# Two attention layers on one core: the layer norms' inverse root as one power on GpSimd

## What is computed

```python
def _ln(x, g, b):
    m = jnp.mean(x, axis=-1, keepdims=True)
    v = jnp.var(x, axis=-1, keepdims=True)
    return (x - m) * jax.lax.rsqrt(v + EPS) * g + b      # EPS = 1e-05

x = _attn(_ln(x, g1, b1), _ln(x, g1, b1), Wq1, Wk1, Wv1, Wo1, bo1) + x
x = _attn(_ln(x, g2, b2), context, Wq2, Wk2, Wv2, Wo2, bo2) + x
x = _geglu_ff(_ln(x, g3, b3), Wp, bp, Wf, bf) + x
```

## Time and profile before

| | |
|---|---|
| median of 3 runs | 3316.51 us (3315.87 to 3318.76) |
| the profiled execution | 3324.0 us, span of its instructions 3322.2 us |
| PE busy | 3117.0 us (94% of the span) |
| DVE busy | 2268.7 us (68%) |
| ACT busy | 1806.2 us (54%) |
| POOL busy | 1168.2 us (35%) |
| mean granted TensorE clock | 0.961 |

### The profile page before, as it was taken

The page is one execution under the profiler, slowest core; times in us unless marked ns, Lnnn a source line. Parts: engine busy times, 40 slices in busy tenths (PEclk is TensorE's granted clock), DMA queues, the critical chain, the costliest instruction groups (busy, mean ns, idle before and its releaser), DMA issues. The chain is left out here.

```text
span 3322.2 us, 48072 instructions
## 1 busy us (share of the span) xinstructions
PE 3117.0 (94%) x16972; PEld 1824.9 (55%) x16972; DVE 2268.7 (68%) x4098; ACT 1806.2 (54%) x3369; POOL 1168.2 (35%) x621
## 2 busy tenths in 40 slices
PE   7989997999989999999999999699888799999989
PEld 5744445788635555555555488543667444444357
DVE  5557873444567777777777465599664799999844
ACT  4445553444434444444444444378655288888864
POOL 2047771000058777877787701012210000000000
PEclk9989998999989999999999999899998699999999
DMA  6989968999976676667666522434726623333140
GB/s 235 346 221 243 244 188 290 361 354 347 294 176 141 149 161 158 148 148 161 158 148 147 195 80 109 165 104 130 261 97 214 208 74 108 92 105 95 58 149 26
DMA packets 367127, 588.79 MB, mean 177 GB/s; under 512 B 47152, under 2 KB 197216, under 8 KB 365736
## 3 DMA queue, kind: packets, MB, share of 16 engines
q1 hardware_dynamic: 361844, 582.43, 59.1%
q10 hardware_dynamic: 5044, 3.29, 0.4%
HBM read 344.19 MB, written 241.29 MB: 176 GB/s over the span
## 5 line engine op out<-in xcount | busy, mean ns | idle before, releaser
L2501 ACT ACTIVATE a_prob<-a_ring 128x512 f32<-128x512 f32 (+1 forms) x1088 | 551.2, 616 | 383.9 <-PE a_ring L2418 371.0
L2266 DVE TENSOR_REDUCE a_blk_max<-a_ring 128x1 f32<-128x402 f32 x992 | 502.1, 569 | 268.8 <-PE a_ring L2257 267.9
L1966 ACT ACTIVATE a_prob<-a_ring 128x512 f32<-128x512 f32 (+1 forms) x1088 | 582.3, 605 | 135.3 <-PE a_ring L1888 130.0
L2365 POOL TENSOR_TENSOR a_prob_sum<-a_prob,a_prob_sum 128x1024 f32<-128x1024 f32 x256 | 604.1, 2399 | 0.0
L2011 DVE TENSOR_REDUCE a_blk_max<-a_ring 128x1 f32<-128x402 f32 x1024 | 506.7, 567 | 33.4 <-PE a_ring L1875 26.6
L2434 PE MATMUL a_pv<-a_prob,a_v 128*64 128x512 f32 (+1 forms) x2176 | 508.6, 606 | 0.0
L2417 PE MATMUL a_ring<-a_q_stack,a_k_stack 128*128 128x512 f32 (+1 forms) x1088 | 454.2, 417 | 18.1 <-issue 12.1
L2418 PE MATMUL a_ring<-a_q_second,a_k_second 65*128 65x512 f32 (+1 forms) x1088 | 435.8, 401 | 0.0
L2365 POOL TENSOR_TENSOR a_prob_sum<-a_prob 128x1024 f32<-128x1024 f32 x128 | 302.7, 2375 | 310.7 <-DVE a_chunk_sum L2558 199.8
L1906 PE MATMUL a_pv<-a_prob,a_v 128*32 128x256 f32 (+2 forms) x4096 | 340.7, 406 | 13.7 <-ACT a_prob L1966 7.8
L1875 PE MATMUL a_ring<-a_k_stack,a_q_stack 63*128 63x402 f32 (+1 forms) x1280 | 281.8, 423 | 37.2 <-DMA a_q_stack<-q_lo_self 17.1
(11 more groups left out here) (278 smaller groups left out, 4875.0 us busy)
## 6 DMA issues: line engine op xcount, KB each, us to landing
a_k_stack<-k_hi_cross SPq DMA_DIRECT2D x96, 400.5 KB, 4.6
a_v<-v_cross SPq DMA_DIRECT2D x48, 768.0 KB
a_k_stack<-k_lo_cross SPq DMA_DIRECT2D x80, 400.5 KB, 5.9
a_k_second<-k_hi_cross SPq DMA_DIRECT2D x32, 801.0 KB, 12.4
v_cross<-p_v_sb SPq DMA_DIRECT2D x48, 512.0 KB
k_hi_cross<-p_split_hi SPq DMA_DIRECT2D x120, 200.0 KB, 3.5
k_lo_cross<-p_split_lo SPq DMA_DIRECT2D x120, 200.0 KB, 4.8
a_q_stack<-q_hi_self SPq DMA_DIRECT2D x64, 256.0 KB, 4.4
```

What stands on the lines that cost most here:

```text
L1966: nc.scalar.activation(prob[0:keys, tau % RC, m, :], ring[0:keys, score_place(e) % BANKS, :], ACT.Exp, scale=a.scale).then_inc(exp_done, 1)
L2266: return nc.vector.reduce_max(dst, bank[:, 0:a.blk], AX.X)
L2365: nc.gpsimd.tensor_tensor(prob_sum[:, h], prob_of(i * NCP + cp, h), other, ALU.add)\
L2501: nc.scalar.activation(prob_of(w, h)[0:keys, ch % 2, :], ring[0:keys, score_bank(e), :], ACT.Exp, scale=a.scale).then_inc(exp_done, 1)
```

## The change

VectorE's reciprocals and ScalarE's square roots are left out of every normalisation. VectorE still adds EPS; GpSimd then waits for that and raises each half of `var` to the power -0.5, with the exponent read from a column of constants, and VectorE's scaling waits for GpSimd's power under the same semaphore (`rooted`) as before. In p0 `fill_constants` now follows the powers of batch 1, where it followed the row sums; in p2 `pad_values` follows the powers of the first normalisation. The exponent column is set in the setup.

```diff
-        self.den_pick = self.sbuf("den_pick", [P, 4], F32)
+        constants = self.sbuf("constants", [P, 5], F32)
+        self.den_pick, self.neg_half = constants[:, :4], constants[:, 4:5]
...
             nc.gpsimd.memset(pr.mean_ones[:], 1.0 / DIM)
+            nc.gpsimd.memset(pr.neg_half, -0.5)
...
                         nc.gpsimd.tensor_tensor(var[:, half], sq[:, 0, half], sq[:, 1, half], ALU.add).then_inc(row_sums, 1)
+                elif kind == "scale":
+                    pool.wait_ge(d_read, d_no["var", m, b] + 1)
+                    for half in HALVES:
+                        nc.gpsimd.tensor_tensor(var[:, half], var[:, half], pr.neg_half.to_broadcast([P, NQ // 2]), ALU.pow)\
+                            .then_inc(rooted, 1)
                     if fill and b == 1:
                         fill_constants()
-            pool.wait_ge(row_sums, 4 * B)
+            pool.wait_ge(rooted, 2 * B)
...
-                elif kind == "scale":
-                    for n, half in enumerate(HALVES):
-                        act.wait_ge(inverted, 2 * b + n + 1)
-                        nc.scalar.activation(var[:, half], var[:, half], ACT.Sqrt).then_inc(rooted, 1)
...
                     nc.vector.tensor_scalar(var[:], d_bank(step), EPS, None, ALU.add).then_inc(d_read, 1)
-                    dve.wait_ge(d_read, d_no[step] + 1)
-                    for half in HALVES:
-                        nc.vector.reciprocal(var[:, half], var[:, half]).then_inc(inverted, 1)
```

```diff
-                elif geglu and kind == "scale" and ln_no[m, b] == 0:
-                    pad_values()
+                elif kind == "scale":
...
+                    if geglu and ln_no[m, b] == 0:
+                        pad_values()
```

More of the change, by code:

```diff
@@ L204, in _ @@
             nc.gpsimd.memset(pr.mean_ones[:], 1.0 / DIM)
+            nc.gpsimd.memset(pr.neg_half, -0.5)
             nc.gpsimd.memset(pr.ident[:], 0.0).then_inc(const_step, 1)
-            nc.gpsimd.memset(pr.den_pick[:], 0.0).then_inc(const_step, 1)
+            nc.gpsimd.memset(pr.den_pick, 0.0).then_inc(const_step, 1)
             pool.wait_ge(const_step, 2)
@@ L209, in _ @@
                                     base=0, pattern=[[-1, P]], channel_multiplier=1).then_inc(const_step, 1)
-            nc.gpsimd.affine_select(out=pr.den_pick[:], in_=pr.den_pick[:], compare_op=ALU.not_equal, fill=1.0,
+            nc.gpsimd.affine_select(out=pr.den_pick, in_=pr.den_pick, compare_op=ALU.not_equal, fill=1.0,
                                     base=-16, pattern=[[-32, 4]], channel_multiplier=1).then_inc(const_step, 1)
@@ L288, in wide_projection @@
     HALVES = [slice(0, NQ // 2), slice(NQ // 2, NQ)]
-    centred, squared, inverted = sem("centred"), sem("squared"), sem("inverted")
+    centred, squared = sem("centred"), sem("squared")
     rooted, scaled = sem("rooted"), sem("scaled")
@@ L984, in feed_phase @@
     x_summed, centred = sem("x_summed"), sem("centred")
-    squared, inverted, rooted, scaled = sem("squared"), sem("inverted"), sem("rooted"), sem("scaled")
+    squared, rooted, scaled = sem("squared"), sem("rooted"), sem("scaled")
     z_hi_done, z_done = sem("z_hi_done"), sem("z_done")
@@ L1480, in _ @@
                         nc.scalar.activation(sq[:, :, half], xc[:, :, half], ACT.Square).then_inc(squared, 1)
[L1481 to L1484, removed]
                 elif kind == "shift":
```

## The result

The changed kernel takes 5372.75 us (median of 4 runs, 5367.96 to 5378.07) against 3317.64 us for the kernel before beside it: a ratio of 1.6175 (95% interval 1.6151 to 1.62). The forecast was 3306.5 us, and its range ended at 3385. The profiled execution has a span of 5367.0 us; the one of before had 3322.2.

What follows compares the result with a forecast made beforehand. TensorE, busy for most of the span, was taken as the bound. Gains of 8.1 us and 5.1 of clock, less 3.5 lost on chains, were rounded to 10: from 3316.5 to 3306.5 us, range 3288 to 3385.

Steps and rivals of the forecast that it cites:

- the price t: Time of one GpSimd power on a 128x256 half, taken as 2.1 us, between 0.74 and 6.1.
- rival 1: The power is long, t about 6: 74 us above the forecast, 3380; slower by over 0.2% had 0.34 in all.
- the formula: In each normalisation's chain, z_lo ends D + 2t + 0.1 + 3.5 us behind the sum with epsilon.
- the v copy: p3 at 2371: a table load and two roots leave from ahead of it, gain 2.0 us, plus 3.4 of clock.
- the mean behind p_x: p3 at 2472: VectorE's residual p_x stands behind the scaling and TensorE waits for its mean; loss 1.1 us.
- the gate: p3 at 2524: a Sqrt load, two roots and a Gelu load leave from ahead of it, gain 2.4 us.
- the second place of 1.1: p3, some 50 us before the place at 2472: the same loss of 1.1 us once more, without slack for TensorE.
- rival 3: The power is as quick as an add, t = 0.74: 25 us gained, 3291.5 us; chance 0.14.
- The loads: p2 to p4: some 35 of ScalarE's table loads for Sqrt and Gelu go, 45 us, mostly hidden behind TensorE.
- The moved fill: p0 at 41.6: the two Wv remainders meet an idle GpSimd, gain 2.6 us, plus 1.7 of clock.
- The port: VectorE instructions with two SBUF operands wait until GpSimd's present instruction ends, so scaling starts at 2t; otherwise 0.83 us less.
- D: VectorE's two-operand instructions between sum and scaling: about 1.1 us for one weight's remainder or two u remainders.

Runs made afterwards that it cites:

- e5: The changed kernel with GpSimd's power on only the first 11 of each half's 256 columns, meant to take 2.1 us each: 3307.56 us, ratio 0.9963.
- e2: The changed kernel with GpSimd multiplying by -0.5 in place of the power, all else the same: 3299.41 us, ratio 0.994.
- e4: The kernel before with ScalarE's square roots made squares, so the table loads for them go; reciprocals and waits stay: 3319.98 us, ratio 0.9997.
- e7: The kernel before without VectorE's reciprocals, ScalarE taking one reciprocal square root in place of its square root; fill constants unmoved: 3302.64 us, ratio 0.9943.
- e3: The kernel before with only GpSimd's fill constants moved, behind the two roots of p0's second normalisation: 3318.44 us, ratio 0.9991.
- e1: The kernel before with eleven GpSimd operations added to its setup, and 24 VectorE multiplications beside the last: 3605.7 us in one run.
- e6: The changed kernel with GpSimd's power on only the first 36 of each half's 256 columns, meant to take 6.1 us each: 3423.84 us, ratio 1.03.
- e8: The kernel before without VectorE's reciprocals, ScalarE taking a logarithm, then an exponential of -0.5 times it, on each half: 3327.67 us, ratio 1.002.

## Why the prediction was wrong, step by step

1. **What failed is the price t.** "I take 2.1 us", between 0.74 and 6.1; it is 41.1. The 2.1 was the sum of what VectorE and ScalarE take for this function, and the upper bound came from how much longer VectorE takes for a reciprocal than for a plain pass (4.1 times), applied twice to GpSimd's add. Nothing in the trace said that GpSimd's price follows those of other engines. A bound that rests on another engine's ratio is no bound. All t above 6.3 had 0.16, and the range stopped short of them. The other half of rival 1 did speak: the Trainium skill, GPSIMD Engine Reference, section Performance pitfalls for Q7 kernels, gives a dependent step as 4 cycles (the 1.2 GHz stand in its section Specifications); by it the measured 0.160 us for a column would be 48 such steps (an estimate), where I had supposed 15. The direction was right and the size a third.
2. **The chain was right as a mechanism, its sum in part by luck.** z_lo waits for the sum, both powers and the rest: 85.8 us measured, 85.9 by the formula, but 0.8 to 1.1 less than the formula where the z_lo are not held up (item 5). At the t that I had taken the sum comes out stage by stage (-9.7 against e5's -10.3), in p3 by terms that miss both ways (e5): the v copy and the mean behind it came out 5.5 us worse than forecast, the mean behind p_x and the gate 4.8 better, and the second place of 1.1 did not show. At t = 0.74 rival 3's 25 us less stands against e2's 21, at 0.6 to 0.7.
3. **The loads went, but were worth little.** 2.0 and 2.4 us in p3 I laid on table loads and roots. e4 takes the loads away and p3 gains 2.1 us; e7 leaves them and p3 gains 4.4 (237.3 against 241.7). At the gate a load less is worth 1.28 us of the idle 2.39 (e4) and the reciprocals 0.81 (e7: 1.58 left); at the v copy what the load frees is lost at the next mean. The share given to the loads was too large.
4. **The moved fill was right** in kind (remainders 1.22 us, idle time and half clock gone) and at its place in size (4.4 against 4.3); over the whole of p0 3.4 are left in e3.
5. **The port was wrong.** "The scaling of both halves starts at 2t": it starts between the powers. The 3.38 us of the earlier trace rows come beside adds; beside a power an instruction of VectorE loses 0.56 us once (e1), 0.35 in the changed kernel (833 ns at most for the scaling, 482 the median). The Trainium skill, GPSIMD Engine Reference, section Specifications, has GpSimd share its SBUF interfaces with VectorE. The adds of the earlier trace rows agree with this; beside a power VectorE is not held for as long as the instruction lasts, and why not, no run shows. So the scaling of the first half and the remainders of D run beside the powers, and the formula is too long by 0.8 to 1.1 us in the chains of p2 and p4 above. At t = 41 this is nothing; at t = 2.1 it turned a loss into a gain: in e5 the p_x of the earlier trace rows starts 5.1 us behind its sum, where 7.1 were forecast and 6.0 stand in the kernel before. The prediction's other sentence, that GpSimd waits where VectorE is first, fits two powers, the first of p2 and of p4, which start beside a weight's remainder and take 42.04 us in place of 41.13.
6. **Rival 1** named the right mechanism. Its point, t = 3, lies between e5's 2.2, where the kernel gains, and e6's 6.2, where it loses; no run is nearer. By its own sum 0.2% slower needs t = 3.5, not 3.4. Its sum at 6.1 us was 66 where e6 shows 102, for it counted too much cover and no half clock.

## What to carry to other kernels

Before an elementwise function is moved to another engine, its price there must come from a run of that very operation: a single instruction in the setup (e1) would have settled this change. Ask next how long the path is from the last matmul to the next one, and shorten that; here it is 28 chains, where 3.4 us of reciprocals less on each are worth 18 us together (e7), and two powers of 41 us cost 73 us on each. A table load costs nothing here while it lies inside its engine's wait; between two dependent operations it puts its full 1.28 us on their path (e8), which costs time where TensorE waits for that path.

## What the runs showed that I had not expected

- GpSimd's power: 0.35 us and 0.160 us for each column, whatever the partitions (16 or 128), base or exponent; its multiply and add of 128x256 take 0.61 and 0.72 us.
- A power of 41 us leaves VectorE's two-operand instructions at 0.41 us, apart from the one at its start (0.97), while adds of 2.4 us make a neighbour wait for nearly a whole one.
- ScalarE's reciprocal square root takes the same 0.41 us as the square root and calls for as many table loads (20 and 18 in p2 to p4); a logarithm followed by an exponential calls for one load each.
